# Routing the two-layer experts inside the last attention slot, with a fixed region of rows for each expert

## What is computed

```
x = x + tanh(g_xattn[2]) * L2_xattn(layernorm(x), ctx)     # 16 heads over 2 x 154 context rows
x = x + tanh(g_ffn[2]) * L2_ffn(layernorm(x))

def L2_ffn(x, Wr, br, W1, b1, W2, b2):       # N_EXP, D, F = 8, 256, 1024
    expert_idx = argmax(x @ Wr.T + br, -1)
    h = relu(einsum('td,efd->etf', x, W1) + b1)
    y = einsum('etf,edf->etd', h, W2) + b2
    return y[expert_idx, arange(tokens)]
```

## Time and profile before

| | before |
|---|---|
| median of 3 runs | 1383.23 us (1382.19 to 1384.61) |
| the profiled execution | 1382.49 us |
| its span | 1380.7 us |
| mean granted clock of PE | 0.918 of full speed |
| busy share of the span | PE 88%, DVE 51%, ACT 32%, POOL 21% |

### The profile page before, as it was taken

The page is one execution under the profiler, slowest core; times in us unless marked ns, Lnnn a source line. Parts: engine busy times, 40 slices in busy tenths (PEclk is TensorE's granted clock), DMA queues, the critical chain, the costliest instruction groups (busy, mean ns, idle before and its releaser), DMA issues.

```text
span 1380.7 us, 19327 instructions
## 1 busy us (share of the span) xinstructions
PE 1218.4 (88%) x6360; PEld 766.8 (56%) x6361; DVE 702.7 (51%) x1997; ACT 448.5 (32%) x842; POOL 292.9 (21%) x347
## 2 busy tenths in 40 slices
PE   6999999999978899999988759999756699999993
PEld 4534434434443444454443649999655556788862
DVE  7273365366984556545652531111176753455557
ACT  3322132223353455444434103333233200333320
POOL 2111111040121111001000041111122564255660
PEclk9999999999988999999998669999977789999997
DMA  9999999100000000000100845555309322455538
GB/s 300 338 338 333 334 334 320 47 31 0 1 1 1 1 1 1 1 1 1 34 1 1 257 145 188 187 183 170 121 20 347 130 92 92 136 168 161 170 112 312
DMA packets 140488, 186.75 MB, mean 135 GB/s; under 512 B 8736, under 2 KB 124960, under 8 KB 140288
## 3 DMA queue, kind: packets, MB, share of 16 engines
q1 hardware_dynamic: 130864, 159.28, 37.3%
q0 software_dynamic: 9552, 26.52, 5.2%
HBM read 83.71 MB, written 102.06 MB: 135 GB/s over the span
## 4 chain that ended last, share of the span: by engine, by line
PE 75%; DVE 12%; ACT 4%; DMA 3%; issue 3%; POOL 2%; SPq 1%; POOLq 0%; DVEq 0%; ACTq 0%
PE psum L2003 14%; PE psum L1266 6%; PE psum L1277 6%; PE psum L2215 5%; PE psum L1055 5%; PE psum L1074 3%; PE psum L936 2%; PE psum L2272 2%; PE psum L2249 2%; PE psum L2296 2%; PE psum L1996 2%; PE psum L2031 2%; PE psum L2193 2%; DVE arena L2834 2%; PE psum L947 2%
## 5 line engine op out<-in xcount | busy, mean ns | idle before, releaser
L2003 PE MATMUL psum<-arena 128*128 128x512 f32 x432 | 204.1, 623 | 0.0
L2834 DVE TENSOR_REDUCE arena<-psum 128x4 f32<-128x616 f32 x128 | 101.6, 797 | 99.2 <-PE psum L2215 98.0
L2003 PEld LDWEIGHTS psum<-arena 128*128 128x128 f32 x432 | 82.4, 197 | 118.5 <-issue 117.7
L2215 PE MATMUL psum<-arena 32*128 32x308 f32 x512 | 105.4, 504 | 16.6 <-DVE arena L2834 15.7
L1182 POOL DMA_INDIRECT ys<-xnT,arena x96 | 92.1, 959 | 91.7 <-DVE xnT L1159 69.1
L2416 ACT ACTIVATE arena<-psum,arena 128x512 f32<-128x512 f32 x72 | 49.0, 685 | 172.8 <-PE psum L2003 163.1
L1894 POOL TENSOR_TENSOR x_tok<-x_tok,add_row 128x1024 f32<-128x1024 f32 x16 | 38.3, 2400 | 269.3 <-ACT xn L1759 269.2
L2507 ACT ACTIVATE arena<-psum 128x2048 f32<-128x2048 f32 x40 | 75.0, 1874 | 59.6 <-PE psum L2253 42.6
L1055 PE MATMUL psum<-arena,xn 128*128 x384 | 87.1, 380 | 2.3 <-ACT xn L1105 1.9
L1266 PEld LDWEIGHTS psum<-side,arena 128*128 128x128 f32 x736 | 87.4, 195 | 2.7 <-ACT side L1311 1.6
L1266 PE MATMUL psum<-side,arena 128*128 128x128 f32 x736 | 87.9, 279 | 1.0 <-ACT side L1311 1.0
(11 more groups left out here) (418 smaller groups left out, 2092.4 us busy)
## 6 DMA issues: line engine op xcount, KB each, us to landing
xs<-zeros SPq DMA_DIRECT2D x8, 8576.0 KB, 60.2
arena<-in_W SPq DMA_DIRECT2D x31, 1024.0 KB, 5.0
xn<-xs SPq DMA_DIRECT2D x64, 134.0 KB, 2.3
arena<-in_gate_up SPq DMA_DIRECT2D x4, 2048.0 KB, 15.7
arena<-xs SPq DMA_DIRECT2D x32, 134.0 KB, 2.4
arena<-in_down SPq DMA_DIRECT2D x4, 1024.0 KB, 14.6
arena<-ys SPq DMA_DIRECT2D x4, 1024.0 KB, 12.7
arena<-ys SPq DMA_DIRECT2D x2, 2048.0 KB, 14.1
```

Of the source, the lines that this page charges most:

```text
L2003: ins = pe.matmul(bank[dict(hn=4, r=5, z=6, xn=7)[k]][:], lhs[:, cols], r, start=(start and n == 0), stop=(stop and n == len(w) - 1))
L2215: ins = pe.matmul(bank[most_bank(n, k) + i][:, 0:2 * M].rearrange("p (h m) -> p h m", h=2), qhT[rows, n % 3, c, t * P:(t + 1) * P], keys[r ...
L2834: dve.tensor_reduce(neg[:, n % 2, t, 2 * pair:2 * pair + 2, 2 * c:2 * c + 2], psum[:, most_bank(n, k):most_bank(n, k) + 2, 0:2 * M].rearra ...
```

## The change

Each of the 8 experts gets a fixed region of 16 tiles (`REGION`) in `xs5`, so a token's row is expert x 2048 + rank, which is known when its own group has been ranked. `xs5` grows from 23 to 129 tiles. The 23 tiles that are computed are found through a table, `first_row5`, from which SP reads the first row of each tile before it loads it. The routing of groups 0, 1 and 2 becomes steps of slot 7 (`r_turn`, `r_logits`, `r_ranks`), that of group 2 partly behind it, and group 3 comes after the slot. Groups 0 to 2 are turned through PSUM banks 4 and 5, group 3 through 2 and 3; the logits lie in bank 4 and the ranks in bank 5. The scatter goes group by group. `hot5_vector` is the one-hot work of one group (bias, maximum, index, one-hot rows, running count), `slots5_vector` the five small steps that give its tokens their rows. The preparation of stage 6 is cut into parts (`single_max_vector`, `single_round_vector` and so on) whose first part stands ahead of the ranks of group 2 on DVE, while its PE products come behind the routing. SP may load the stage 6 matrices and six of the eight `W2` pieces before stage 4 is done.

```diff
             yield ("weigh", n, 4)
+            yield from routed("r_turn", 0)
...
             yield from behind("back", n - 1, 1)
+            yield from routed("r_logits", 0)
...
             yield from behind("project", n - 1, 1)
+            yield from routed("r_turn", 1)
...
             yield ("values", n, 1)
+            yield from routed("r_ranks", 0)
...
             yield ("weigh", n, 2)
+            yield from routed("r_logits", 1)
...
             yield ("values", n, 3)
+            yield from routed("r_ranks", 1)
...
-            yield from (("back", n, 0), ("back", n, 1), ("project", n, 0), ("project", n, 1))
+            yield from (("r_turn", 2), ("back", n, 0), ("back", n, 1), ("project", n, 0), ("project", n, 1), ("r_logits", 2))
```

```diff
+        def turn5_tensor(pe, g):
+            pe.wait_ge(*xn_ready.at(5, g + 1))
+            if g == 0:
+                pe.wait_ge(most_found, 16 * SLOTS)
+            elif g == 1:
+                pe.wait_ge(*logits_read.at(5, 1))
+            elif g == 2:
+                pe.wait_ge(*logits_read.at(5, 2))
+                pe.wait_ge(*slots_ready.at(5, 2))
+            else:
+                pe.wait_ge(weighed, weighed_at[SLOTS - 1, 3] + 1)
...
+        def slots5_vector(dve, ch, g):
+            dve.wait_ge(*ranks_done.at(5, g + 1))
+            ch.step(dve.scalar_tensor_tensor(r["place"], iota_e[:, 0:E2].unsqueeze(1).broadcast_to([P, GT, E2]), float(REGION * P),
+                                             bank[5][:, 0:GT * E2].rearrange("p (t e) -> p t e", t=GT), ALU.mult, ALU.add))
...
                 elif op[0] == "normalise":
                     finish(op[1])
+                elif op == ("r_turn", 2):
+                    finish(5)
+                elif op[0] == "r_logits":
+                    if op[1] == 2:
+                        finish(5)
+                    hot5_vector(dve, ch, op[1])
+                    if op[1] == 2:
+                        single_max_vector(dve, ch)
+                elif op[0] == "r_ranks":
+                    slots5_vector(dve, ch, op[1])
...
-                route_tensor(pe, 5, wr5, (w5_loaded, 4 * 16), free=lambda: pe.wait_ge(*x_done.at(4, G)))
+                turn5_tensor(pe, G - 1)
+                ranks5_tensor(pe, G - 2)
+                logits5_tensor(pe, G - 1)
+                ranks5_tensor(pe, G - 1)
+                single_max_turn(pe)
+                start_tensor(pe, 5)
+                tiles_tensor(pe, 5)
+                single_max_spread(pe)
+                single_keys_tensor(pe)
                 single_context_tensor(pe)
                 expert_tiles_tensor(pe)
...
-                route_vector(dve, ch, 5, br5)
+                slots5_vector(dve, ch, G - 2)
+                hot5_vector(dve, ch, G - 1)
+                slots5_vector(dve, ch, G - 1)
+                tiles_vector(dve, ch, 5)
+                passed_vector(dve, ch, 5)
+                rows5_vector(dve, ch)
+                single_round_vector(dve, ch)
                 single_context_vector(dve, ch)
...
-                sp.dma_start(xs5.rearrange("(t p) d -> p t d", p=P),
-                             zeros[:, 0:D5].unsqueeze(1).broadcast_to([P, NT2, D5])).then_inc(zeroed, 16)
+                for n, first in enumerate(range(0, SPARE5 + 1, 64)):
+                    many = min(64, SPARE5 + 1 - first)
+                    sp.dma_start(xs5[first * P:(first + many) * P].rearrange("(t p) d -> p t d", p=P),
+                                 zeros[:, 0:D5].unsqueeze(1).broadcast_to([P, many, D5])).then_inc(zeroed, 16)
...
-                sp.dma_start(xin[:, u], xs5[bass.ds(i * P, P), :]).then_inc(in_loaded[u].sem, 16)
+                row = sp.value_load(first_row5[0:1, bass.ds(i, 1)], min_val=0, max_val=SPARE5 * P)
+                sp.dma_start(xin[:, u], xs5[bass.ds(row, P), :]).then_inc(in_loaded[u].sem, 16)
```

327 lines of the change are left out of this document (164 added, 163 removed).

## The result

The changed kernel takes 1376.15 us (median of 14 runs, 1359.3 to 1381.4) where the kernel before takes 1383.2 us on the same chip (14 runs, 1376.4 to 1390.5). The ratio is 0.9916, interval 0.9887 to 0.9945: faster by 0.8%, where 0.5% was forecast. The medians of all runs lie 7.05 us apart, which is 0.5%. The changed kernel's profiled execution took 1370.08 us, its span is 1368.5.

What follows compares the result with a forecast made beforehand. PE bounds the expert tiles, which can only begin earlier. Gains of 5.4 us at the first tile and 2.0 in its products take 1382.5 to 1375.1; with 0.7 to the median, 1375.8 us, range 1369.5 to 1383.

Steps and rivals of the forecast that it cites:

- What is late next: Before the first expert tile: the preparation of stage 6 ends last, at 816.1, with the scattered rows in by 808.
- the first products: First expert tile: its hidden products, 5.62 us before, get 2.0 us shorter because PE comes from products without a gap.
- the slot: Slot 7, with routing steps put in: 13.9 us longer, its last `project` ending at 779.9 instead of 766.0.
- the way behind it: From slot 7's last `project` to the first expert tile: 36.2 us instead of 55.5.
- signs of being wrong: Granted clock under 0.9 in 740 to 765, a DMA releasing the first tile, or expert tiles over 7.25 us each.
- the clock's term: Slot 7: the clock falls once, while DVE finishes group 2's norm, slowing sixteen transposes and part of `project`: 2.5 us.
- the walk: Slot 7, step by step on three engines: the delays that the inserted routing steps add sum to 11.4 us.
- the one-hot work of group 1: Slot 7, on DVE ahead of the first `untangle`: it delays the slot by 2.3 us.
- the turning of group 2 with its wait: Slot 7, ahead of `back`: the rest of group 2's norm, the turning on PE and a wait add 3.0 us.
- 4.9 us and a table read later: After the last scatter begins at 802.3: the first tile's rows are in by 808, leaving 8 us of slack.
- The zeroing: SP's queue: 14.1 MB more takes 45 us more, hidden with 7 us or more left before POOL needs the weights.
- half clock through the second half of the slot: Rival: all products there double, 20 to 22 us of delay instead of 11.4; 1382 to 1384, no change; chance 0.11.

Runs made afterwards that it cites:

- before_again: The kernel before the change, profiled and measured once more with no edit: ratio 0.9998 to before.
- hot1_late: Changed kernel with DVE's one-hot work of group 1 moved from ahead of slot 7's first `untangle` to behind its second: ratio 0.9933 to before.
- turn2_behind: Changed kernel with group 2's turning moved from ahead of slot 7's `back` steps to behind its last `project`: ratio 0.9890 to before.
- prep_early: Changed kernel with the preparation of stage 6 spread between the routing's steps behind the slot: ratio 0.9953 to before.
- max_late: Changed kernel with DVE's fills and maxima for stage 6 moved from behind group 2's one-hot work to behind group 3's places: ratio 0.9967 to before.
- w1_late: Changed kernel with the first two loads of W1 issued behind the first two loads of scattered rows instead of ahead: ratio 0.9956 to before.
- before_zero: Kernel before the change with only the larger `xs5` and its zeroing, 129 tiles in three transfers instead of 23 in one: ratio 1.0008 to before.
- all_behind: Changed kernel with nothing routed in the last slot, all four groups behind its last `project`, fixed regions kept: ratio 0.9893 to before.
- kept_busy: Changed kernel with PE's idle stretches filled by small products whose results nobody reads: ratio 0.9967 to before.

## Why the prediction was right

The sum had 7.4 us, and the traces show 7.7 (6.2 and 1.8 to 2.3 by the repeats). What is late next and the first products were foreseen. That the sum came out so near is in part luck: the slot cost 2.5 us more than predicted and the way behind it 3.0 less. Of the prediction's signs of being wrong one came true, a granted clock under 0.9 in 740 to 765 (0.88), and the slot is longer by 16.4 us, outside the 11 to 15 that were to show it right. Point by point:

- **The slot**: 13.9 us longer predicted, 16.4 measured. The step that failed is the clock's term, "2.5 us". PE is busy in the slot for 15.0 us more than before (40.18 against 25.17), of which two logits, three turnings and two sets of ranks take 7.5 at the full clock (2 x 1.95 + 3 x 1.04 + 2 x 0.25) and 1.3 are group 2's logits at the window's end. I put the other 6.2 us down to the low clock (an estimate). Some 1.1 of them are the slot's start, which isn't the change's doing: before_again, whose slot starts at the low clock too, takes 31.6 us. So about 5.1 us stand against the 2.5 of the term, since the clock was down in four stretches and not in one. The rest of the delay was then 10.2 us (16.4 - 6.2) where the walk had 11.4. Of its terms, the one-hot work of group 1 measured 1.9 instead of 2.3 (hot1_late), and the turning of group 2 with its wait 4.0 instead of 3.0 (turn2_behind against prep_early).
- **The way behind it**: 36.2 predicted, 33.2 measured. The rows of group 3 were ready 15.9 us behind the last `project` instead of 17.0 (the one-hot work took 2.5 us, not 2.7, and the maxima 3.3, not 3.5). From there to the keys' product it was 5.8 us instead of 6.5, and the products and copies took 11.4 instead of 12.7, because the first two sets, which took 4.47 and 2.75 us before, now took 4.05 and 1.89. The maxima were on DVE's chain, as the sum has them, but PE's chain beside them was as long (max_late).
- **What is late next**: the preparation of stage 6, shown by the bracket of the first tile and by prep_early, which moved it and moved the tile. The slack of the scatter was predicted at 8 us and is 2, because the step "4.9 us and a table read later" left out that two loads of 1 MB run beside the last scatters (w1_late). The scatters are issued one per 1.27 us, as before.
- **The first hidden products**: 2.0 predicted, 1.8 measured.
- **The zeroing** is hidden (before_zero). SP's queue reaches the weights behind it at 281.65 us instead of 239.99, 41.7 us later where 45 were counted; POOL is at its work at 295.14 us where it was at 301.17, with no wait for a weight.
- **What the prediction didn't ask** is whether the move into the slot pays. Its own numbers had the answer: the slot costs 13.9 us and the way behind it gains 19.3, but 5.4 of these are the scatter's wait, which goes without the move too, and what is left is 13.9. all_behind shows it: 79.5 against 80.1.

The rival "half clock through the second half of the slot" was partly what happened (a mean of 0.82 over the slot, with one of the falls ahead of its second half), but its 20 to 22 us of delay were not reached (16.4), and the way behind was 3 us shorter than predicted.

## What to carry to other kernels

When a change has two parts, here fixed regions and work moved into an earlier stage, price them apart: the part that lets each group be sent at once took away the wait, while the moved work, by the one trace in which it stands behind the slot instead, paid for itself and no more. Work put into a stretch in which PE waits for others wasn't free here: it cost much of its own time, and the stretch lost the full clock. And two profiles that differ by 12 us may owe 7 of it to the code ahead of the change; compare by marks around the change, and repeat the unchanged kernel. The same holds for an experiment: look whether the time that it gains lies where its edit acts, before adding it to another's.

## What was not expected of the hardware

- The granted clock falls in stretches in which PE is busy all the time: 0.50 over 736 to 742 in the changed kernel, 6.00 of 6 us busy, and 0.50 over 793 to 799 in kept_busy. It follows no rule that these runs show; the same code had another pattern in another run. Slots of the same code were 46.9 us in three runs and 49.1 in two (prep_early, max_late). Those two started at the full clock, but their last `project` took 5.57 and 5.59 us instead of 3.72, and they hold a stop of ACT (next point).
- In the twelve traces of the experiments engines stand idle for some microseconds with a releaser that the profile calls remote; the two first traces have none. Most are in stage 7's loops. The view of waits of before_again (engine, buffer and line waited for: us in total, times, longest):

```profile
ACT arena L1113 <- remote: 24.1, 8, 3.4
DVE xnT L1159 <- remote: 17.2, 7, 2.9
```

One stands in the last slot of prep_early, max_late, kept_busy and turn2_behind, in all four at the same place: ACT goes on 0.53 to 0.54 us ahead of the second `rests`. That speaks against a disturbance by chance, but no run looks for its cause. In prep_early's timeline ACT begins the exponential of `weigh` 3 only here, 1.8 us after PE had ended it (761.05):

```profile
762.89 1.88 ACT L2545 ACTIVATE arena<-psum 128x2048 f32<-128x2048 f32 x1 [4.01 <-remote]
```

Behind the first tile these traces take 571 to 579 us against 559 and 560 in the first two. The stops may be most of the 16 us between the chips, but no run tried it. Where they come from stays open.
